# Four graph layers on one core: the preparation of the weights placed among the parts of the first LSTM turn, and the edge softmax done in four pieces inside one block with the edge-logits and the aggregation

## What is computed

```
A: h = relu(adj @ (h @ Wg0 + bg0)); h = relu(adj @ (h @ Wg1 + bg1))
   for p in 1..4:  an LSTM runs over windows of p nodes (own weights Wih[p-1], Whh[p-1]);
                   its last hidden state replaces the last node of each window
B: causal attention: softmax(q k^T/sqrt(C) + adj) v, @ Wo
C: out_i = adj_ii h_i W[0] + sum_{j>i} adj_ij h_j W[1] + sum_{j<i} adj_ij h_j W[2] + bias
D: Xq, Xv = h @ W_lin.T, h @ W_val.T (4 heads of 32)
   e  = sum_d a * leaky_relu(Xq[src] + Xq[dst]) + log(adj[src,dst] + 1e-8)      # 256 edges
   attn = softmax of e over the edges with the same src
   Y[src] += attn * Xv[dst];  out = Y @ W_out.T
```

## Time and profile before

| | us |
|---|---|
| median of 3 runs (1250.34 to 1251.29) | 1250.83 |
| the profiled execution, its own time | 1249.93 |
| its span, first to last instruction | 1248.2 |
| granted TensorE clock over the span, mean | 0.988 |
| PE busy | 1177.1 (94%) |
| DVE busy | 1006.7 (81%) |
| ACT busy | 813.5 (65%) |
| POOL busy | 401.6 (32%) |

### The profile page before, as it was taken

One profiled execution on the slowest core, in us unless ns is written; L12 is line 12 of the kernel. 1 busy time (PEld: TensorE's weight loads), 2 busy tenths in 40 slices (PEclk: granted clock), 3 DMA queues, 4 the chain that ended last, 5 costly groups with the idle time before them and its releaser, 6 DMA issues. The chain is left out here.

```text
span 1248.2 us, 24592 instructions
## 1 busy us (share of the span) xinstructions
PE 1177.1 (94%) x7808; PEld 1024.5 (82%) x7808; DVE 1006.7 (81%) x2796; ACT 813.5 (65%) x1804; POOL 401.6 (32%) x779
## 2 busy tenths in 40 slices
PE   2899999999999999999998999989999799959998
PEld 2689898898988989889897888877777688838997
DVE  6698888988889888898886899977776677766775
ACT  4487685876858768588585777767776477732332
POOL 3100000000000000000001677756664788813332
PEclk9999999999999999999998999999999899979999
DMA  9300000000000000000000000000000000001222
GB/s 270 109 1 1 2 1 1 0 0 0 0 0 0 0 0 0 0 0 0 1 2 1 2 2 2 2 2 1 1 1 1 1 2 2 2 1 51 75 67 76
DMA packets 24728, 21.09 MB, mean 17 GB/s; under 512 B 1744, under 2 KB 20304, under 8 KB 24400
## 3 DMA queue, kind: packets, MB, share of 16 engines
q1 hardware_dynamic: 24656, 20.21, 5.6%
HBM read 11.82 MB, written 8.39 MB: 16 GB/s over the span
## 5 line engine op out<-in xcount | busy, mean ns | idle before, releaser
L573 ACT ACTIVATE gate<-ps,b_lstm 128x256 f32<-128x256 f32 (+2 forms) x624 | 309.6, 564 | 96.6 <-PE ps L600 95.1
L598 PE MATMUL ps<-H_hi,w_hi 128*128 128x256 f32 (+2 forms) x624 | 210.0, 338 | 0.0
L599 PE MATMUL ps<-H_hi,w_lo 128*128 128x256 f32 (+2 forms) x624 | 205.7, 331 | 0.0
L600 PE MATMUL ps<-H_lo,w_hi 128*128 128x256 f32 (+2 forms) x624 | 193.2, 330 | 0.0
L126 POOL TENSOR_SCALAR rstd<-mv 128x8 f32<-128x8 f32 x18 | 5.8, 322 | 569.6 <-DVE mv L107 569.5
L598 PEld LDWEIGHTS ps<-H_hi,w_hi 128*128 128x128 f32 x624 | 117.8, 189 | 12.9 <-DVE H_lo L510 3.5
L599 PEld LDWEIGHTS ps<-H_hi,w_lo 128*128 128x128 f32 x624 | 117.9, 189 | 7.8
L600 PEld LDWEIGHTS ps<-H_lo,w_hi 128*128 128x128 f32 x624 | 115.7, 189 | 10.2 <-DVE H_lo L548 1.5
L598 PE MATMUL ps<-hid_hi,w_hi 128*128 128x256 f32 (+2 forms) x384 | 121.3, 322 | 0.0
L599 PE MATMUL ps<-hid_hi,w_lo 128*128 128x256 f32 (+2 forms) x384 | 117.4, 312 | 0.0
L600 PE MATMUL ps<-hid_lo,w_hi 128*128 128x256 f32 (+2 forms) x384 | 106.7, 319 | 0.6
(11 more groups left out here) (206 smaller groups left out, 3131.3 us busy)
## 6 DMA issues: line engine op xcount, KB each, us to landing
out<-x SPq DMA_DIRECT2D x32, 256.0 KB, 2.3
w_raw<-in_WihT SPq DMA_DIRECT2D x1, 1024.0 KB, 8.2
w_raw<-in_WhhT SPq DMA_DIRECT2D x1, 1024.0 KB, 8.4
wqkvT<-in_WqkvT SPq DMA_DIRECT2D x1, 192.0 KB, 5.2
w_sb<-in_W SPq DMA_DIRECT2D x1, 192.0 KB, 4.8
ends_row<-in_src_row SPq DMA_DIRECT2D x1, 128.0 KB, 3.6
ends_row<-in_dst_row SPq DMA_DIRECT2D x1, 128.0 KB, 3.8
x<-in_x_in SPq DMA_DIRECT2D x8, 0.5 KB, 10.4
```

The lines of the kernel that those rows point to most:

```text
L573: nc.scalar.activation(gate[:, g, z, 0:w * GB], gate_bank(g, k, m)[:, 0:w * GB], ACT.Tanh if z == G else ACT.Sigmoid, bias=b_lstm[:, 4 * ( ...
L598: nc.tensor.matmul(dst, w_hi[:, src, p - 1, z], v_hi, start=start, stop=False)
L599: return nc.tensor.matmul(dst, w_lo[:, src, p - 1, z], v_hi, start=False, stop=False)
L600: return nc.tensor.matmul(dst, w_hi[:, src, p - 1, z], v_lo, start=False, stop=stop)
```

## The change

The preparation block is gone. Its loads, products and splits are inserted in the LSTM block's first turn; the edge tables are built in stage C; the softmax pieces lie in stage D's and E's common block. In particular:

- Loads: SP issues batches 0 to 3, adjT, batches 4 to 7, w_g and bg1, batches 8 to 15, the p = 1 slice of Wih (256 KB), batches 16 to 31, the other LSTM weights (0.75 MB each; the p = 1 slice of Whh is not loaded, it is not used), then the rest. The raw LSTM weights land in the room of batches 96 to 127, which are loaded when all `w_lo` are made. Four small loads are issued by ACT. `dst_row` is no longer loaded.
- The layernorm sums of half a come first on DVE, in two parts of four batches; those of half b follow. Ranking of the edges is spread over DVE's parts of the first turn, and the sort is one product of ones with `moved`.
- ACT splits the weights in seven instructions of 512 elements per partition, ahead of its first A1 part; all seven low parts are POOL's. PE waits for the low parts that a step needs.
- A0 of a later turn waits for 2 or 1 gates less of the turn before (banks 0 and 1 come free earlier).
- D and E are one block, unrolled. `lr` has two buffers, and PE makes two groups' logits at every second group. The softmax of set k (8 groups) is spread over the seven groups that follow the set: one group each for sums and scans, maximum and subtraction, exponential, transpose, copy, sum over sources, reciprocal and product. The fourth set's pieces lie in the first eight groups of the aggregation. Four accumulations of logits use two banks in turn, bank 7 holds the transposes and the sums.

```diff
+    def part(i, g, what, k, m, _):                                    # ACT
+        if opening(i) and (what, k, g) == (A0, 0, 1):
+            act.wait_ge(S["o_shift"], 3)
+            relu_norm(act, 0, 1, 0, GB)
+        if opening(i) and (what, k, g) == (A1, 0, 0):
+            for n, (src, p) in enumerate(SPLITS):
+                act.wait_ge(*((S["ld_lstm"], n_lstm) if n else (S["ld_w1"], 16)))
+                nc.scalar.activation(w_hi[:, src, p], raw_of(src, p), ACT.Copy).then_inc(S["w_high"], 1)
...
+    pool.wait_ge(S["ld_w"], n_w)                                      # POOL
+    link(nc.gpsimd.affine_select(out=adj_causal[:], in_=adj_sb[:], ...))
+    for k, (src, p) in enumerate(SPLITS):
+        pool.wait_ge(S["w_high"], k + 1)
+        nc.gpsimd.tensor_tensor(w_lo[:, src, p], raw_of(src, p), w_hi[:, src, p].bitcast(F32),
+                                ALU.subtract).then_inc(S["w_low"], 1)
...
+    if opening(i) and what in (SHARE, HIGH):                          # PE
+        pe.wait_ge(S["w_low"], splits_of(steps[k][0]))
...
-    pe.wait_ge(sa(g, "a_gate"), i * TG)
+    pe.wait_ge(sa(g, "a_gate"), i * TG - CH + k)
...
+    def stage(i, what, g, more, before):                              # C, DVE
+        if what == STATS2 and isinstance(i, int) and i in (0, TURNS - 1):
+            edge_tables(g if i == 0 else W1 + g)
...
+SUMS, LESS, EXPS, TURN, TAKE, TOTAL, SHARES = range(1, 8)
+def due(n, what):
+    k, at = (n - PER) // PER, (n - PER) % PER
+    return k if 0 <= k < BH and at == what else None
...
     for n in range(NG):                                               # D, DVE
         dve.wait_ge(S["d_xqh"], n + 1)
         nc.vector.tensor_tensor(xq_lo[:], by4(ps[:, 1]), xq_hi[:].bitcast(F32), ALU.subtract)
         if n + 3 < NG:
             norm_sums(n + 3)
+        softmax(n)
         for k in range(2):
             dve.wait_ge(S["d_rl"], n * 2 + k + 1)
-            if k == 0 and n > 0:
-                dve.wait_ge(S["d_lgp"], n)
+            if k == 0 and n > 1:
+                dve.wait_ge(S["d_lgp"], n - 1)
             nc.vector.scalar_tensor_tensor(lr[:, n % 2, ...], ps[:, 3 + k], SLOPE, rl[:, k], ...)
...
-                    if n > 0:                                         # D, PE
+                    if n % 2 == 0 and n > 0:
+                        logits(n - 2)
                         logits(n - 1)
+                    softmax(n)
                     pe.wait_ge(S["d_xqh"], n + 1)
                     pe.wait_ge(S["d_xql"], n + 1)
+                    if n > 0:
+                        pe.wait_ge(S["d_lr"], n * 2)
...
+    values(0)                                                         # E, PE
+    logits(NG - 2)
+    logits(NG - 1)
+    for n in range(NG):
+        aggregate(n)
+        if n + 1 < NG: values(n + 1)
+        project(n)
+        softmax(NG + n)
```

More of the change, by code:

```diff
@@ L366, in four_layers, with splits_of, opening @@
+        SPLITS = [(0, 0)] + [(src, p) for p in range(1, SKIPS) for src in range(2)]
+        n_e, n_g, n_w, n_lstm, n_late = 4 * 16, 3 * 16, 3 * 16, 4 * 16, 5 * 16
+        def splits_of(p):
+            return 1 + SPLITS.index((min(p - 1, 1), p - 1))
+        def opening(i):
+            return isinstance(i, int) and i == 0
         CH = GB * T // 512
@@ L492, in part, with turn_part @@
+                def turn_part(i, g, what, k, m, before):
                     if what == OUT:
@@ L1042, in _ @@
                                                 ALU.mult, ALU.add).then_inc(S["d_hn"], 1)
+                for n in range(NG):
+                    pool.wait_ge(S["e_xvh"], n + 1)
+                    nc.gpsimd.tensor_tensor(xv_lo[:], xv[:, n * QB:n * QB + QB, :].rearrange("p b c -> p (b c)"),
+                                            xv_hi[:].bitcast(F32), ALU.subtract).then_inc(S["e_xvl"], 1)
             @block.vector
@@ L1076, in _, with finish @@
+                def finish(n):
+                    xs = x[:, n * QB:n * QB + QB, :]
+                    dve.wait_ge(S["e_op"], n + 1)
+                    nc.vector.tensor_tensor(xs, xs, by4(ps[:, 3]), ALU.add).then_inc(S["e_o"], 1)
+                weigh(0)
+                for n in range(1, NG):
+                    weigh(n)
+                    finish(n - 1)
+                    softmax(NG + n - 1)
+                finish(NG - 1)
             @block.scalar
@@ L1099, in _, with high_values, copy_y @@
                             S["d_rl"], 1)
+                def high_values(n):
+                    act.wait_ge(S["d_xv"], n + 1)
+                    if n > 0:
+                        act.wait_ge(S["e_vp"], n * EC)
+                        act.wait_ge(S["e_xvl"], n)
+                    nc.scalar.activation(xv_hi[:], xv[:, n * QB:n * QB + QB, :].rearrange("p b c -> p (b c)"),
+                                         ACT.Copy).then_inc(S["e_xvh"], 1)
+                def copy_y(n):
+                    act.wait_ge(S["e_yp"], n + 1)
+                    if n > 0:
+                        act.wait_ge(S["e_op"], n)
+                    nc.scalar.activation(y3[:], by4(ps[:, 2]), ACT.Copy).then_inc(S["e_y"], 1)
+                high_values(0)
+                high_values(1)
+                for n in range(NG):
+                    copy_y(n)
+                    if n + 2 < NG:
+                        high_values(n + 2)
+                    exponentials(NG + n)
             @block.tensor
```

740 lines of the change are left out of this document (385 added, 355 removed).

## The result

The changed kernel took 1218.19 us in the median, against 1251.05 for the kernel before: ratio 0.9736, 95% interval 0.9718 to 0.9753. The profiled execution took 1217.63 us, its span is 1214.2. (One execution of four took 2348.75 us; it has no part in the ratio.) Forecast were 1220.5 and a range of 1208 to 1235.

What follows compares the result with a forecast made beforehand. PE bounds the kernel except in the opening and between last Z and first aggregation. Terms -24.5 + 0.8 - 2 - 19.8 + 2.7 + 10.2 + 2.0 = -30.6, plus 0.3, give a median of 1220.5 us, range 1208 to 1235.

Steps and rivals of the forecast that it cites:

- The opening: Start of the kernel: first LSTM product at 25.0 us in place of 51.9; term -24.5 us, ends -29 and -16.
- rival of late weights: Opening: last LSTM weight lands 8 us later than 17, LSTM starts 6 to 8 later, 1228 us; chance 0.16.
- A0's release: Later LSTM turns: A0 needs two or one gates less, of 5.0 us waited; -2 us, ends -5 and 0.
- The boundary: Last Z to first aggregation: about 6.1 us in place of 25.9; -19.8 us, ends -21 and -17.
- The edge-logit stage: First to last Z: +2.7 us for unequal groups and +10.2 for softmax pieces put inside, together +12.9.
- SUMS: Edge-logit stage, group with softmax sums and scans on DVE: next Z at 5.05 against 4.42, 0.63 us a set.
- LESS: Edge-logit stage, group after the sums, 0.9 us on DVE: moves a Z from 3.62 to 4.2, 0.58 us.
- SHARES: Edge-logit stage, reciprocal over 256 elements (1.6 us) and product (0.6) on DVE: 1.1 us of delay a set.
- Stage C: Edge tables built there, some 17 DVE instructions beside a full PE: +0.8 us, ends 0 and +2.
- the aggregation: Fourth softmax set lies there: 1.2 us of PE and 0.8 of delay, +2.0 us, ends +1.2 and +4.
- POOL holds DVE: Rival: five two-input DVE pieces a set each wait 0.5 to 1 us for POOL, +4 a set, 1232 us; chance 0.14.
- DVE holds POOL: Rival: denser DVE work stretches POOL's edge-logit group over 5.28 us, kernel slower, 1261 us at 5.6; chance 0.03.

Runs made afterwards that it cites:

- Experiment 3: Changed kernel with batches 8 to 15 issued right behind batches 4 to 7, LSTM weights and batches 16 to 31 only after they land: 1213.89 us, ratio 0.9702.
- experiment 8: Changed kernel with half b's load first, W0 before half b's A0, POOL's low parts later, log chain ahead of the joint block's groups, shares split: 1210.83 us, ratio 0.9682.
- experiment 1: Kernel before with one edit, A0 waiting only for the gate that last used its own bank: 1242.6 us, ratio 0.994.
- experiment 6: Changed kernel with the log chain ahead of the joint block's first group and one small Exp behind the Ln: 1216.76 us, ratio 0.9728.
- experiment 2: Kernel before with only the new joint block of edge-logits and aggregation, adj kept in SBUF: 1244.04 us, ratio 0.9946.
- experiment 4: Changed kernel with half b's first A0 put behind half a's second W0 on PE, first turn only: 1218.28 us, ratio 0.9738.
- experiment 5: Changed kernel with POOL's seven low parts held back until DVE's four ranking pieces are done: 1216.88 us, ratio 0.9736.

## Why the prediction was right, and where it was not

The total was right to 2.3 us, and that is in good part luck: two large terms were wrong by 7 us each, in opposite directions. The mechanism was right at the boundary and in the edge-logit stage, and wrong in what bounds the opening and in the size of A0's wait.

**The opening was mis-sized: -24.5 forecast, -17.5 measured.** The step that failed is "From A0's start to the first LSTM product the old trace takes 51.92 - 37.50 = 14.4 us". A0 started at 9.13 as forecast (about 10), but the first product came 23.5 us later. The old trace has both halves' batches in SBUF when A0 begins. In the new one half b's shift, put at "about 13.8", came at 17.1, since its batches landed at 11.7: they are the seventh load that SP issues, behind adjT and the three small arrays, with the weights right behind them, and I had gone by the megabytes in the queue and asked only when the weights would be there. Then comes the clock, for which I had taken "nothing": PE ran at 0.51 from 17 to 23.5 us, 1.7 us of the chain. Experiment 3 shows both: 4.8 of the 7.0 us come back with that load ahead of the weights. The new first turn is 1.9 us longer than the old one in the changed kernel and 1.8 in experiment 3, of which the forecast had at most its 2.5 for DVE; with all three edits of the opening (experiment 8) the term is -23.3. The rival of late weights named the wrong load; ACT's splits did come late behind half b's scaling (24.74 for about 18), but the first LSTM product waited for DVE. The 1.5 for DVE beside POOL had the right size (2.27 for 0.73 us).

**A0's release was mis-sized: -2 forecast, -8.9 measured**, outside its ends of -5 and 0. I took the waits view's 5.0 us for an upper bound and took 3 off for a wait for ACT's copy. The 5.0 isn't a bound, since it counts from modelled ends, and the wait for the copy doesn't come: experiment 1 gives -8.5 for the edit alone, with A0 0.12 us behind its neighbour in every turn.

**The boundary was right: -19.8 against -19.9**, with 1.5 us of luck in it: of the nine kernels with this boundary two take 5.94 us, at a clock of 1.00, one 6.41 and six 7.2 to 7.7, where the clock falls in PE's wait of 2.65 us for POOL's low part (0.53 and 0.59 behind it in experiments 3 and 8).

**The edge-logit stage: +12.9 forecast, +8.7 measured.** The beat is 7.90 a pair for 8.04. SUMS costs 0.24 for 0.63 and LESS 0.25 for 0.58: the delay of `lr` doesn't pass on whole, probably because ACT's rl and the next `xq_hi` go on beside it, which no run tests. PE's moved work was right (1.1 for 1.2), SHARES 0.74 for 1.1. Against that stand the two things that I had not costed at all, the log chain and the table load, 1.65 us in three distances, which experiment 6 takes out one by one; and 0.9 before the first Z.

**Stage C +1.5 for +0.8, the aggregation +1.5 for +2.0:** inside their ends. Experiments 1 and 2 show that the first is the tables' own.

**The rival "POOL holds DVE" is out for powers and all but out for scalings, but the two engines do hold each other.** The scans and the subtraction take 0.69, 0.67 and 0.42 beside a POOL that is busy 104.6 of 130 us (the subtraction 0.48 beside a scaling). It is POOL that waits beside them:
```profile
994.73 0.64 POOL L1113 TENSOR_SCALAR shift<-mv 128x4 f32<-128x4 f32 x1
995.34 1.42 POOL L1115 TENSOR_TENSOR rstd<-rstd,half 128x4 f32<-128x4 f32 x1
```
The first step takes 0.23 elsewhere and the power 1.04, and beside the maximum two scalings take 0.74 and 0.75 for 0.46. In the kernel before, whose DVE has no instruction with two SBUF inputs in this stage, none of these is longer (a scaling 0.49 at most). And a scan can be held, as the kernel before shows at its boundary:
```profile
1106.69 1.40 POOL L1179 TENSOR_TENSOR xv_lo<-xv,xv_hi 128x512 fp32r<-128x512 f32 x1 [11.41 <-ACT xv_hi L1248]
...
1106.95 1.69 DVE L1193 TENSOR_TENSOR_SCAN bwd<-cut_b,lgs 128x256 f32<-128x256 f32 x1
```
By the rule of the Trainium skill, "SBUF — State Buffer", section "Who interferes with whom", a two-input DVE instruction and a POOL instruction that reads SBUF exclude each other, the second waiting until the first is through. The traces agree where DVE came first, and where POOL's wide two-input subtraction did; they don't for a power of POOL under way, beside which DVE's products of two SBUF inputs keep their 0.69 us in every turn. The rival "DVE holds POOL" has its mechanism, then, but not its price: some 1.1 us of POOL a set of eight groups, where it needed 0.95 a group, and PE doesn't wait for POOL in this stage.

## What to carry to other kernels

Where an engine's list goes on with the other half of the data, the first thing that it waits for sets everything behind it: follow each load to the first instruction that needs it, also the one that isn't the large one. Take lost time from start to start of neighbouring instructions, not from a waits view whose ends are modelled; here that was 7.5 us for 5.0. Where DVE and POOL both read SBUF, look at the lengths of both: the one that is held may be the one with time to spare. And after a stretch in which PE idles, price the next steps at both clock levels: each stage start here is worth 1 to 2.7 us either way, which is as much as many an edit, so a single profile of an edit elsewhere can show it as the edit's own.

## What the runs showed of the hardware that was not expected

- ACT's table loads of 1.28 us: the Ln in the stage cost two of them, its own and one for the Exp after it. One small Exp right behind the Ln moved the second to where ACT had nothing to do.
- The granted clock at a stage's start after PE idled for 1.5 to 6.3 us: at stage C it was 1.00 in experiment 1 and fell to 0.50 in experiment 2, with the same code of that stage and the same idle time of 1.5 us ahead of it, and so again for the changed kernel (1.00) and experiment 4 (0.50). It also differs between executions of one kernel: the kernel before had a mean clock of 0.974 to 0.988. The price was 1.9 to 2.3 us there, 2.7 in stage B, 1.5 at the boundary. It stayed at 1.00 in every place where unread products filled the gap.
- A DVE instruction with one wide input (two of 256 elements, 0.73 us) took 2.27 beside POOL's wide subtraction of two SBUF inputs; experiment 5 moved the subtraction away and had 0.73.
- DVE's scans made a power of POOL 1.42 us long for 1.04, and a small POOL step 0.64 for 0.23; a POOL power under way didn't lengthen DVE's products.
